# Row maxima of attention scores: one VectorE reduction over two PSUM banks, two such pairs and three ScalarE banks in place of three and four single ones

## The chip, the cores and the metric

One Trainium2 chip, one core of it. The metric is the device time of one execution in microseconds (us). The engines are TensorE (PE in the profile, PEld for its weight loads), VectorE (DVE), ScalarE (ACT), GpSimd (POOL) and SyncE (SP, which here issues transfers). The results of matrix products land in PSUM, which has 8 banks of 128 partitions x 512 f32 values. VectorE and ScalarE read them from there.

## The reference, cut to what matters

A differential attention layer followed by a routed feed-forward layer, each with a residual and a layer norm. The change touches the attention part alone:

```python
# x: 8 batches x 512 tokens x 128; 16 heads, 8 key/value heads, head size 4, two score maps per head
s = einsum('bthd,bshd->bhts', q, k) * scale
s = where(causal mask, s, most negative)
p = softmax(s, axis=-1)                        # needs the row maximum for safety
attn = einsum('bhts,bshd->bthd', p, v)
attn = attn1 - lambda_full * attn2             # then RMS norm, @ Wo, residual, layer norm
```

Behind it every token goes to one of 8 experts (the one with the largest router logit), and tokens are sorted by expert and run through the expert's weights in slots of 256 rows.

## The kernel before, in words

**Two passes over the scores.** The softmax subtracts each row's maximum before the exponential. So every score is computed twice: once with queries on the partitions ("natural", for the maxima, line 1393 on VectorE), and once with keys on the partitions ("turned", for the exponential, line 910 on ScalarE), where the maxima are fed into the product as extra rows of an operand. The maxima of a stage go VectorE (L1402, L1403: the maxima of pairs of halves, `mt`) -> GpSimd (split into three bf16 parts, `msplit`) -> TensorE (transposed, L743, the use `turn_max`) -> ScalarE (`mturn`) -> a transfer to memory and back into `qd`.

**Phases, steps and units.** The work of one batch is cut into 4 stages (`SUPER`), 32 stages in all (`NS`). In phase g the kernel takes the maxima of stage g and the exponentials of stage g - 2 (`LAG`). A phase has 9 steps t (`NC`), each of two units u = 2t and 2t + 1 (`NU` = 18). A unit is one PSUM bank of natural scores and one of turned scores, 128 x 512 each: a causal mask (L624 or L627 natural, L651 or L654 turned) and one or two products on top (L633 and L642 natural, L660 and L669 turned). The two units of a step use the upper and lower half of TensorE's rows and overlap partly. Behind the two units of a step TensorE takes the other uses of that step (list `uses(g, t)`) and the products of probabilities and values (L712, the "products").

**Three sets of banks.** The natural scores rotate through 3 banks (`NAT_RING`), which VectorE empties; three small uses that VectorE reads take a place in that rotation too (`wo`, `router`, `rank`). The turned scores rotate through 4 banks (`ST_RING`), which ScalarE empties, with `turn_max`, `turn_ot`, `turn_attn`, `turn_x1`, the projections `q`, `q2`, `k`, `k2` and `v` in the same rotation. The eighth bank (`pv_b`) gathers the products. TensorE waits before each filling until the bank's earlier content has been read: `s_nfree` counts VectorE's, `s_sfree` ScalarE's. TensorE takes its instructions in the written order, so a wait for either holds everything behind it.

**The jobs between.** VectorE's small work for a batch that is through with attention (`jobs_at`: `weigh`, `guess`, `stats`, `choose`, `chance`, `place`) is laid out by hand, one job after each unit's maximum. Most `choose`, `chance` and `place` jobs wait by semaphore for the job before them.

**What repeats.** With 4 stages to a batch, four kinds of phase follow one another. They are named here by what stands in them:

- phase with k (g = 5, 9, ...; for g = 21 VectorE's part lies at 324.42 to 340.24 us): projection `k` at step 2, `k2` at step 6, `wo` at step 8;
- phase with v (g = 22: 340.24 to 353.86 us): `stats` in steps 0 to 2, `v` at step 2, `weigh` in steps 5 and 6;
- phase with the router (g = 23: 353.86 to 368.46 us): `router` at step 2, `guess` from step 2 to 4, `choose` from step 4 to 8;
- phase with q (g = 20: 310.97 to 324.42 us, and g = 24: 368.46 to 381.91 us): `chance` at step 0, `rank` at step 2, `place` in steps 4 and 5, `q`, `q2` and `turn_attn`.

Every phase has `turn_max` at step 2 and `turn_ot` at step 4, and products in steps 0, 1, 3, 5, 6, 7 and 8.

After the 34 phases the feed-forward part runs over 23 slots; it uses the same eight banks under fixed numbers, and the change does not touch it.

## Time and profile before

| what | value |
|---|---|
| time, median of 3 runs | 680.28 us (674.95 to 680.87) |
| time of the profiled execution | 670.18 us |
| its span, first to last instruction | 667.7 us |
| busy: PE, DVE, ACT, POOL | 593.7, 539.6, 433.3, 415.3 us |
| TensorE clock granted, mean | 0.952 of full speed |
| phase with k, v, router, q (from one `mt` maximum to the next) | 15.82, 13.62, 14.60, 13.45 us |
| maxima of 128x512 (L1393) | 576, 369.2 us busy |
| exponentials of 128x512 (L910) | 576, 313.5 us busy |

A busy time counts when an engine had an instruction in work; VectorE's and ScalarE's records overlap a little with the next one, so the time from start to start is shorter than the record. The span is 2.5 us shorter than the time of the same execution. The time of the profiled execution stands 10 us under the median of the runs.

### The profile page before, as it was taken

How to read it: one execution, taken by the hardware profiler on the slowest of the kernel's cores; microseconds unless marked ns; L12 is line 12 of the kernel's file. 1: busy time of each engine (PE TensorE's matmuls, PEld its weight loads, DVE VectorE, ACT ScalarE, POOL GpSimd, SP SyncE). 2: the span in 40 equal slices, each digit the busy share in tenths (PEclk: the TensorE clock that was granted, in tenths of full speed). 3: DMA queues.
4: the chain of work that ended last, by engine and by line, in shares of the span. 5: the costliest groups of instructions: out<-in, count | busy, mean ns of one | idle time of the engine just before them, and what ended most of it. 6: DMA issues, size and time to landing. Idle time of an engine off the chain costs nothing.

```text
span 667.7 us, 19245 instructions
## 1 busy us (share of the span) xinstructions
PE 593.7 (89%) x6968; PEld 330.2 (49%) x6968; DVE 539.6 (81%) x1318; ACT 433.3 (65%) x903; POOL 415.3 (62%) x618
## 2 busy tenths in 40 slices
PE   3389899999989999998999999999988896999990
PEld 1134344344434444443444444343445785999990
DVE  6488988998998998899899889999746975666661
ACT  1105788887978887797888779787875343444441
POOL 6245257566877676687777668336363367687774
PEclk9576999999999999999999999999979996999995
DMA  3867566555664756666465655634129446465530
GB/s 112 262 211 246 159 197 217 165 177 183 186 197 123 231 162 190 202 183 194 113 229 167 213 190 166 192 115 117 46 60 329 138 137 189 136 196 189 196 125 24
DMA packets 70677, 114.54 MB, mean 172 GB/s; under 512 B 20028, under 2 KB 43068, under 8 KB 70300
## 3 DMA queue, kind: packets, MB, share of 16 engines
q1 hardware_dynamic: 58152, 76.22, 37.5%
q0 software_dynamic: 9168, 34.25, 14.9%
q10 hardware_dynamic: 3264, 2.85, 1.3%
q8 instruction: 55, 0.90, 0.6%
q14 instruction: 38, 0.31, 0.2%
HBM read 69.60 MB, written 47.27 MB: 175 GB/s over the span
## 4 chain that ended last, share of the span: by engine, by line
PE 53%; DVE 26%; DMA 6%; issue 6%; ACT 3%; POOL 2%; SPq 1%; ACTq 0%; POOLq 0%; DVEq 0%
DVE mr L1393 15%; PE bank L712 11%; PE bank L840 11%; PE bank L852 4%; PE bank L624 4%; PE bank L642 4%; PE bank L633 3%; DMA rows<-qk_parts 3%; PE bank L720 2%; PE bank L749 2%; PE bank L660 2%; PE bank L669 2%; PE bank L723 2%; ACT work L910 1%; PE bank L759 1%
## 5 line engine op out<-in xcount | busy, mean ns | idle before, releaser
L1393 DVE TENSOR_REDUCE mr<-bank 128x8 f32<-128x512 f32 x576 | 369.2, 681 | 43.7 <-PE bank L642 26.8
L910 ACT ACTIVATE work<-bank 128x512 f32<-128x512 f32 x576 | 313.5, 602 | 72.5 <-PE bank L669 51.4
L712 PE MATMUL bank<-work,v_aug 128*32 128x512 f32 (+7 forms) x2048 | 170.9, 418 | 0.0
L642 PE MATMUL bank<-rows 64*128 64x384 bf16 (+7 forms) x512 | 144.1, 292 | 0.0
L633 PE MATMUL bank<-rows 64*128 64x128 bf16 (+7 forms) x512 | 140.9, 293 | 0.0
L669 PE MATMUL bank<-qd,kz 64*128 64x384 bf16 (+7 forms) x512 | 137.0, 286 | 0.0
L660 PE MATMUL bank<-qd,kz 64*128 64x128 bf16 (+7 forms) x512 | 133.8, 287 | 0.0
L624 PE MATMUL bank<-bits 64*128 64x128 bf16 x448 | 100.8, 227 | 9.6 <-DVE mr L1393 8.6
L624 PEld LDWEIGHTS bank<-bits 64*128 64x128 bf16 x448 | 41.8, 94 | 121.5 <-DVE mr L1393 107.3
L651 PE MATMUL bank<-bits 64*128 64x128 bf16 x448 | 97.3, 224 | 0.0
L840 PE MATMUL bank<-xr,rows 128*128 128x256 f32 x368 | 86.6, 390 | 5.2 <-DVE xr L1619 4.6
L840 PEld LDWEIGHTS bank<-xr,rows 128*128 128x128 f32 x368 | 70.3, 196 | 15.0 <-DVE xr L1619 5.1
L1024 ACT ACTIVATE apart<-bank 128x256 f32<-128x256 f32 x92 | 34.6, 382 | 58.0 <-PE bank L840 42.5
L712 PEld LDWEIGHTS bank<-work,v_aug 128*32 128x32 f32 x2048 | 45.0, 108 | 49.1 <-issue 21.5
L1103 POOL CAST msplit<-mt 128x32 bf16<-128x32 f32 x32 | 7.7, 240 | 90.1 <-DVE mt L1403 90.1
L1239 POOL DMA_INDIRECT out_dram<-kz,row_u x46 | 45.4, 987 | 14.0 <-issue 10.4
L1655 DVE TENSOR_TENSOR apart<-apart,bank 128x256 f32<-128x256 f32 x92 | 37.2, 418 | 18.0 <-ACT apart L1024 17.3
L660 PEld LDWEIGHTS bank<-qd,kz 64*128 64x128 bf16 x512 | 47.5, 96 | 6.0
L1184 POOL DMA_INDIRECT x_sorted<-x_all,pos_u x32 | 32.0, 1000 | 29.4 <-DVE pos_u L1483 21.9
L642 PEld LDWEIGHTS bank<-rows 64*128 64x128 bf16 x512 | 49.4, 97 | 0.3 <-issue 0.3
L633 PEld LDWEIGHTS bank<-rows 64*128 64x128 bf16 x512 | 48.7, 96 | 0.5 <-issue 0.2
L669 PEld LDWEIGHTS bank<-qd,kz 64*128 64x128 bf16 x512 | 47.2, 95 | 1.2
(177 smaller groups left out, 1006.1 us busy)
## 6 DMA issues: line engine op xcount, KB each, us to landing
qk_apart<-apart SPq DMA_DIRECT2D x54, 256.0 KB, 3.6
rows<-qk_apart SPq DMA_DIRECT2D x64, 192.0 KB
kz<-qk_apart SPq DMA_DIRECT2D x64, 192.0 KB
qk_parts<-parts SPq DMA_DIRECT2D x90, 128.0 KB, 2.9
qk_apart<-apart POOLq DMA_DIRECT2D x42, 256.0 KB, 3.9
rows<-qk_parts SPq DMA_DIRECT2D x64, 96.0 KB
qd<-qk_parts SPq DMA_DIRECT2D x64, 96.0 KB
x_sorted<-in_c_pad SPq DMA_DIRECT2D x9, 390.0 KB, 4.3
```

Source lines behind the costliest of these rows:

```text
L624: pe.matmul(bk[:, :].rearrange("p (n t) -> p n t", t=L)[:, NB - 1 - i:NB:i, :], ident_h[lo:lo + L, :], mask_h[lo:lo + L, :], start=True, s ...
L633: m = pe.matmul(bk[:, 0:wa], qz[lo:lo + L, kv, NB - 1 - i].rearrange("p j l -> p (j l)"), kd[lo:lo + L, kv, 0:wa], start=False, stop=True, ...
L642: pe.matmul(bk[:, wa:T], qz[lo:lo + L, kv, i - 1].rearrange("p j l -> p (j l)"), kd[lo:lo + L, kv, 0:T - wa], start=False, stop=True, skip ...
L651: pe.matmul(bk[:, :].rearrange("p (n t) -> p n t", t=L)[:, 0:NB - i + 1:NB - i, :], ident_h[lo:lo + L, :], turned_h[lo:lo + L, :], start=T ...
L660: m = pe.matmul(bk[:, 0:wa], kz[lo:lo + L, kv, i].rearrange("p j l -> p (j l)"), qd[lo:lo + L, kv, L * i:T], start=False, stop=True, skip_ ...
L669: pe.matmul(bk[:, wa:T], kz[lo:lo + L, kv, NB - i].rearrange("p j l -> p (j l)"), qd[lo:lo + L, kv, wa:T], start=False, stop=True, skip_gr ...
L712: m = pe.matmul(pv_b[32 * t:32 * t + 32, L * kb:T], v_aug[:, vb, kv + v, kb, :], cols, start=kb == 0, stop=True, skip_group_check=True)
L840: m = pe.matmul(banks[f][:, h * SLOT:(h + 1) * SLOT], wbuf[:, n, h * FFN + f * P:h * FFN + (f + 1) * P], xst[:, n % 2, :], start=h == 0, s ...
L910: nc.scalar.activation(prob[:, pos, r, :], st_b[no % ST_RING][:, :], ACT.Exp, scale=HD ** -0.5).then_inc(s_sfree, 1)
L1239: nc.gpsimd.indirect_dma_start(out=out, out_offset=bass.IndirectOffsetOnAxis(row_u[:, j, a:a + 1], 0), in_=ynorm[:, j % 2, a, :], in_offse ...
L1393: V.tensor_reduce(mr[:, s % 2, u % 2, i, i:i + NB], nat_b[no % NAT_RING][:, :].rearrange("p (n t) -> p n t", t=L), AX.X, ALU.max)\
L1655: V.tensor_tensor(u_s[:, j % 2, f, :], sa[:, f, :], banks[f][:, SLOT:2 * SLOT], ALU.mult)\
```

## The change

Four of the eight banks become two pairs, each one PSUM tensor of 128 x 2 x 512. The two units of a step go to the two halves of a pair, and one reduction takes the maxima of both. TensorE waits for a free pair before the first unit of a step only. The rotation of natural scores then has 2 places (each a pair) in place of 3, that of turned scores 3 in place of 4. A use by VectorE (`wo`, `router`, `rank`) takes a whole place, of which it fills one bank. VectorE's order changes with it: the maximum of both units, then the uses of the step, then both jobs of the step.

```diff
         for t in range(NC):
             if g < NS:
-                for u in (2 * t, 2 * t + 1):
-                    nat["max", g, u] = len(nat_at)
-                    nat_out += 1
-                    nat_at.append(nat_out)
+                nat["max", g, t] = len(nat_at)
+                nat_in += 2
+                nat_out += 1
+                nat_filled.append(nat_in)
+                nat_at.append(nat_out)
...
-NAT_RING, ST_RING = 3, 4
+NAT_RING, ST_RING = 2, 3
...
-        banks = [bank(f"bank{i}") for i in range(8)]
-        nat_b, st_b, pv_b = banks[0:3], banks[3:7], banks[7]
+        nat_b = [ctx.enter_context(nc.psum_tensor(f"pair{i}", [P, 2, 512], F32)) for i in range(NAT_RING)]
+        st_b, pv_b = [bank(f"bank{i}") for i in range(ST_RING)], bank("products")
+        banks = [pair[:, r, :] for pair in nat_b for r in range(2)] + st_b + [pv_b]
...
-                    nat_wait(pe, NAT_NO["max", g, u])
+                    if u % 2 == 0:
+                        nat_wait(pe, NAT_NO["max", g, u // 2])
                     nat_mask(g, u)
...
-                wait(dve, s_nat, no + 1)
-                V.tensor_reduce(mr[:, s % 2, u % 2, i, i:i + NB],
-                                nat_b[no % NAT_RING][:, :].rearrange("p (n t) -> p n t", t=L), AX.X, ALU.max)\
+                wait(dve, s_nat, NAT_IN[no])
+                V.tensor_reduce(mr[:, s % 2, :, i, i:i + NB],
+                                nat_b[no % NAT_RING][:, :, :].rearrange("p r (n t) -> p r n t", t=L), AX.X, ALU.max)\
                     .then_inc(s_nfree, 1)
...
-                for u in range(NU):
+                for t in range(NC):
                     if g < NS:
-                        row_max(g, u)
-                    if u % 2:
-                        for name, n in uses(g, u // 2):
-                            take(name, n)
-                    for name, b, k in jobs_at(g, u):
-                        job(name, b, k)
+                        row_max(g, t)
+                    for name, n in uses(g, t):
+                        take(name, n)
+                    for u in (2 * t, 2 * t + 1):
+                        for name, b, k in jobs_at(g, u):
+                            job(name, b, k)
```

On VectorE, in a phase with the router, from the router's logits to the `choose` jobs (steps 2 to 5; `ss`, `nv`, `nint`, `rinv` are the `guess` jobs, `rmax`, `less`, `coded` the first `choose` jobs). Before:

```order
L1418 TENSOR_TENSOR logit<-bank,rb_s 128x32 [waits s_rt,s_nat]
L1362 TENSOR_SCALAR ss<-ss 128x64 [waits s_ss]
L1393 TENSOR_REDUCE mr<-bank 128x8 [waits s_nat]
L1365 TENSOR_SCALAR nv<-ss 128x64 [waits s_ss]
L1393 TENSOR_REDUCE mr<-bank 128x8 [waits s_nat]
L1367 TENSOR_SCALAR nint<-ss 128x64
L1393 TENSOR_REDUCE mr<-bank 128x8 [waits s_nat]
L1371 TENSOR_SCALAR rinv<-nint 128x64 [waits s_newton]
L1393 TENSOR_REDUCE mr<-bank 128x8 [waits s_nat]
L1444 TENSOR_REDUCE rmax<-logit 128x4 [waits s_nfree,s_rt]
L1393 TENSOR_REDUCE mr<-bank 128x8 [waits s_nat]
L1447 TENSOR_TENSOR less<-logit,rmax 128x32 [waits s_rexp,s_rt]
```

The same stretch now:

```order
L1433 TENSOR_TENSOR logit<-pair,rb_s 128x32 [waits s_rt,s_nat]
L1374 TENSOR_REDUCE ss<-sq 128x64 [waits s_newton,s_post]
L1377 TENSOR_SCALAR ss<-ss 128x64 [waits s_ss]
L1408 TENSOR_REDUCE mr<-pair 128x2x8 [waits s_nat]
L1380 TENSOR_SCALAR nv<-ss 128x64 [waits s_ss]
L1382 TENSOR_SCALAR nint<-ss 128x64
L1408 TENSOR_REDUCE mr<-pair 128x2x8 [waits s_nat]
L1386 TENSOR_SCALAR rinv<-nint 128x64 [waits s_newton]
L1459 TENSOR_REDUCE rmax<-logit 128x4 [waits s_nfree,s_rt]
L1408 TENSOR_REDUCE mr<-pair 128x2x8 [waits s_nat]
L1462 TENSOR_TENSOR less<-logit,rmax 128x32 [waits s_rexp,s_rt]
L1465 TENSOR_TENSOR coded<-logit,rmax 128x32 [waits s_rt]
```

Two jobs now follow one another where each had a maximum ahead of it; `ss` (L1377) stands right behind the sum that it reads, and `coded` (L1465) right behind the `choose` job that it waits for by semaphore.

On TensorE, in a phase with v, from `turn_max` at step 2 to the two units of step 3. Before:

```order
L743 MATMUL bank<-bits,msplit 96x128 [waits s_msp,s_sfree]
L730 MATMUL bank<-wv_s,xt_s 128x64 [waits s_sfree]
L730 MATMUL bank<-wv_s,xt_s 128x64 x3
L624 MATMUL bank<-bits 128x2x64 [waits s_nfree]
L651 MATMUL bank<-bits 128x128 [waits s_sfree]
L633 MATMUL bank<-rows 128x64
L660 MATMUL bank<-qd,kz 128x64
L642 MATMUL bank<-rows 128x448
L669 MATMUL bank<-qd,kz 128x448
L624 MATMUL bank<-bits 128x2x64 [waits s_nfree]
L651 MATMUL bank<-bits 128x128 [waits s_sfree]
```

The same stretch now (`pair` is a natural bank, `bank` a turned one):

```order
L758 MATMUL bank<-bits,msplit 96x128 [waits s_msp,s_sfree]
L745 MATMUL bank<-wv_s,xt_s 128x64 [waits s_sfree]
L745 MATMUL bank<-wv_s,xt_s 128x64 x3
L638 MATMUL pair<-bits 128x2x64 [waits s_nfree]
L665 MATMUL bank<-bits 128x128 [waits s_sfree]
L647 MATMUL pair<-rows 128x64
L674 MATMUL bank<-qd,kz 128x64
L656 MATMUL pair<-rows 128x448
L683 MATMUL bank<-qd,kz 128x448
L638 MATMUL pair<-bits 128x2x64
L665 MATMUL bank<-bits 128x128 [waits s_sfree]
```

No matrix product moved. The second unit of a step no longer waits for VectorE, and each wait on `s_sfree` is now for the third place back where it was for the fourth.

## Rows read from the trace of the kernel before

**Rows 1.** The page, costliest groups: busy, mean ns of one, idle before.

```profile
L1393 DVE TENSOR_REDUCE mr<-bank 128x8 f32<-128x512 f32 x576 | 369.2, 681 | 43.7 <-PE bank L642 26.8
...
L624 PEld LDWEIGHTS bank<-bits 64*128 64x128 bf16 x448 | 41.8, 94 | 121.5 <-DVE mr L1393 107.3
```

**Rows 2.** Windows of four phases: k, v, router, q.

```profile
324.42:340.24 15.82, 15.82 (x233) 7.73 (x236) 12.85 (x23) 12.56 (x26) 11.33 (x17) 1.00 0.59 189
340.24:353.86 13.62, 13.15 (x181) 6.21 (x181) 13.30 (x32) 12.29 (x26) 11.73 (x16) 1.00 0.55 169
353.86:368.46 14.60, 13.89 (x191) 6.05 (x185) 14.55 (x34) 11.80 (x25) 10.21 (x21) 1.00 0.58 173
368.46:381.91 13.45, 12.31 (x183) 5.74 (x184) 12.13 (x26) 10.22 (x22) 9.29 (x12) 1.00 0.67 216
```

**Rows 3.** Groups by shape, VectorE: the same operation at two widths.

```profile
L1580 DVE TENSOR_TENSOR at<-on_s,rl 128x1024 f32<-128x1024 f32 x1 | 1.2, 1225 | 0.0
...
L1584 DVE TENSOR_TENSOR dif<-at 128x512 f32<-128x512 f32 x1 | 0.7, 693 | 0.0
```

**Rows 4.** Timeline of VectorE, behind the last maxima: start, duration.

```profile
479.53 0.18 DVE L1469 TENSOR_REDUCE rsum<-chance 128x4 f32<-128x32 f32 x1
479.74 0.18 DVE L1471 RECIPROCAL x_all<-rsum 128x4 f32<-128x4 f32 x1
```

**Rows 5.** Timeline of ScalarE, phase with k: exponentials of units 4-5 and 8-9.

```profile
328.60 1.08 ACT L910 ACTIVATE work<-bank 128x512 f32<-128x512 f32 x2
...
331.98 1.08 ACT L910 ACTIVATE work<-bank 128x512 f32<-128x512 f32 x2 [0.57 <-PE bank L669]
```

**Rows 6.** Timeline of TensorE, the same phase: `k`, unit 6, products of step 3, unit 11.

```profile
328.81 0.64 PE L720 MATMUL bank<-xr,wq_s 128*32 128x256 f32 x8
...
329.82 0.23 PE L651 MATMUL bank<-bits 64*128 64x128 bf16 x1
...
330.47 1.07 PE L712 MATMUL bank<-work,v_aug 128*32 128x512 f32 x8
...
332.99 0.22 PE L651 MATMUL bank<-bits 64*128 64x128 bf16 x1
```

**Rows 7.** Timeline of ScalarE, phase with v: exponentials of units 6 to 9.

```profile
346.18 2.07 ACT L910 ACTIVATE work<-bank 128x512 f32<-128x512 f32 x4
```

**Rows 8.** Timeline of TensorE, phase with v: turned masks of units 10 and 11.

```profile
347.42 0.23 PE L651 MATMUL bank<-bits 64*128 64x128 bf16 x1
...
347.81 0.23 PE L651 MATMUL bank<-bits 64*128 64x128 bf16 x1
```

**Rows 9.** Timeline of VectorE, phase with v, units 8 to 17 and `weigh`.

```profile
346.53 2.06 DVE L1393 TENSOR_REDUCE mr<-bank 128x8 f32<-128x512 f32 x3 [0.20 <-PE bank L642]
...
350.75 3.07 DVE L1393 TENSOR_REDUCE mr<-bank 128x8 f32<-128x512 f32 x5
353.86 0.29 DVE L1402 TENSOR_REDUCE mt<-mr 128x16 f32<-128x128 f32 x1
```

**Rows 10.** Timeline of VectorE, phase with the router, steps 6 to 8.

```profile
365.05 0.17 DVE L1455 TENSOR_REDUCE rtop<-place_f 128x4 f32<-128x32 f32 x1
365.15 0.68 DVE L1393 TENSOR_REDUCE mr<-bank 128x8 f32<-128x512 f32 x1
...
367.75 0.68 DVE L1393 TENSOR_REDUCE mr<-bank 128x8 f32<-128x512 f32 x1
368.46 0.29 DVE L1402 TENSOR_REDUCE mt<-mr 128x16 f32<-128x128 f32 x1
```

**Rows 11.** Timeline of VectorE, start of the phase with q.

```profile
310.97 0.29 DVE L1402 TENSOR_REDUCE mt<-mr 128x16 f32<-128x128 f32 x1
...
311.36 0.68 DVE L1393 TENSOR_REDUCE mr<-bank 128x8 f32<-128x512 f32 x1
```

**Rows 12.** Timeline of TensorE, start of the phase with q.

```profile
309.70 0.20 PE L627 MATMUL bank<-bits 64*128 64x64 bf16 x1 [0.49 <-DMA rows<-qk_parts]
...
315.62 1.06 PE L712 MATMUL bank<-work,v_aug 128*32 128x512 f32 x8
```

More of the change, by code:

```diff
@@ L424, in place, with filled @@
             if (name, n) in TAIL_NO:
[L425 removed]
+                return pv_b, TAIL_NO[name, n], s_tail, s_tfree
             if name in FOR_DVE:
[L427 to L428 removed]
+                return nat_b[NAT_NO[name, n] % NAT_RING][:, 0, :], NAT_NO[name, n], s_nat, s_nfree
+            return st_b[ST_NO[name, n] % ST_RING], ST_NO[name, n], s_st, s_sfree
+        def filled(eng, name, n):
+            if (name, n) in TAIL_NO:
+                eng.wait_ge(s_tail, TAIL_NO[name, n] + 1)
+            elif name in FOR_DVE:
+                eng.wait_ge(s_nat, NAT_IN[NAT_NO[name, n]])
+            else:
+                eng.wait_ge(s_st, ST_NO[name, n] + 1)
         def emptied(eng, name, n):
@@ L521, in row_operands @@
                 if s >= SUPER:
-                    wait(sp, s_nat, NAT_NO["max", s - SUPER, NU - 1] + 1)
+                    wait(sp, s_nat, NAT_IN[NAT_NO["max", s - SUPER, NC - 1]])
                 if dst is qz:
@@ L733, in use @@
             def use(name, n):
-                bk, done, no, _ = place(name, n)
+                bk, no, done, _ = place(name, n)
                 if (name, n) in TAIL_NO:
@@ L924, in take @@
                     return
-                bk, done, no, free = place(name, n)
-                wait(act, done, no + 1)
+                bk, _, _, free = place(name, n)
+                filled(act, name, n)
                 if name == "v":
@@ L1226, in _ @@
                     if g == PHASES - 1 and t == 5:
-                        wait(pool, s_nat, NAT_NO["max", NS - 1, NU - 1] + 1)
+                        wait(pool, s_nat, NAT_IN[NAT_NO["max", NS - 1, NC - 1]])
                         pool.wait_ge(s_es, 1)
@@ L1407, in take @@
                     return
-                bk, done, no, free = place(name, n)
-                wait(dve, done, no + 1)
+                bk, _, _, free = place(name, n)
+                filled(dve, name, n)
                 if name == "wo":
```

23 lines of the change are left out of this document (11 added, 12 removed).

## The prediction

> **What bounds the kernel now.** I read the costliest groups first. VectorE's maxima are 576 instructions and 369.2 us, and the largest idle time ahead of a natural mask on TensorE (107.3 us of PEld) ends with a maximum [rows 1]. That suggests VectorE. The windows of one batch's four phases correct this picture [rows 2]. With k, TensorE is busy for all of its 15.82 us and VectorE for 12.85: TensorE bounds it. With the router, VectorE is busy for 14.55 of 14.60. With v it is busy for 13.30 of 13.62, and TensorE for 13.15, so both are nearly full. With q neither is (12.13 and 12.31 of 13.45): the reader will see below that VectorE holds its first third and TensorE the rest. The four make 57.49 us, with TensorE busy for 55.16 and VectorE for 52.84. So even free maxima could take no more than 2.3 us from a batch. The granted clock is 1.00 in all four, and the change gives no reason to move it. The rest of the argument is who is late where, phase by phase.
>
> **What one merged maximum costs.** A single maximum has a record of 0.68 us, and five in a row take 3.07 [rows 9]: (3.07 - 0.68) / 4 = 0.60 us from start to start. The trace has no reduction of 1024 elements. Another VectorE operation goes from 693 to 1225 ns when its row goes from 512 to 1024 elements, 0.53 us more [rows 3]. So the merged record is 0.68 + 0.53 = 1.21 us and the distance to the next one 0.60 + 0.53 = 1.13, where two singles took 1.20. The saving is 0.07 us a pair, 0.63 us a phase of nine. The bounds are 0 (the fixed part was hidden by overlap anyway) and 2 x 0.681 - 1.215 = 0.147 us (it wasn't); I take 0.07, since it goes by distances, which is what a full engine lives by.
>
> The Trainium skill (VectorE: DVE Perf Modes, on the trn2 errata) says that memory latency is exposed between instructions, and that one large tile pays it once where many small ones pay it each time. Its table has 120 cycles at 0.96 GHz as the fixed part of a reading from PSUM, 0.125 us. By the page the pairs would save 288 x 0.125 = 36 us of VectorE, by the distances 288 x 0.07 = 20; the sum below goes by the distances.
>
> **What two jobs in a row cost.** A small job between two maxima moves the next one by 0.10 us (365.05 to 365.15) [rows 10]: its latency lies under the maximum behind it. A job that waits for the one directly before it starts 0.21 us after it [rows 4]. So every waiting second job costs 0.11 us more than it did between two maxima. I count four in the phase with the router (`ss` behind its sum, `choose` 2, 4, 6), one with v (`stats` 4), two with q (`chance` 1, `place` 1), none with k. An independent second job costs nothing more.
>
> **What the third ScalarE bank costs.** TensorE may fill a turned bank when ScalarE has read what stood there, now three places back. I set each filling against the end of the reading three places earlier; a start came 0.05 us behind the releasing end where TensorE waited before.
>
> With k, step 2: the places are units 4, 5, `turn_max`, `k`. The exponential of unit 4 ends at 328.60 + 0.60 = 329.20 [rows 5], `k` starts at 328.81 [rows 6]. It would have to wait until 329.25: 0.44 us. At step 5, unit 11 starts at 332.99 [rows 6], and unit 9 is read at 331.98 + 1.08 = 333.06 [rows 5]: 0.12 us. TensorE is full in this phase, so both go into its length: **+0.56 us**. Elsewhere in this phase a filling starts after that end. The bound below is zero, if ScalarE gets back ahead through its idle 0.57 us [rows 5]; but what it waits for there is TensorE.
>
> With q, unit 11 repeats the 0.12 us. With the router the same place is hidden, since TensorE waits for VectorE all the time.
>
> **Phase with v.** ScalarE is late here: it empties `v` in four pieces and reads units 6 to 9 from 346.18 to 346.18 + 2.07 = 348.25 [rows 7]. Unit 11 was filled from 347.81 [rows 8], under a rotation of four. Under three its turned mask starts at 348.30, and its natural products, which stand behind that mask on TensorE, end about 0.45 later (unit 10: mask at 347.42 [rows 8], maximum at 346.53 + 2.06 - 0.68 = 347.91 [rows 9]), at 348.75. The maximum of units 10 and 11 can't start before, where that of unit 10 alone started at 347.91: 0.84 us late, of which 0.39 is the second half of the pair (347.42 to 347.81) and the rest the bank. `v` itself must wait like `k` does; it moves the chain by about 0.1 more (estimate). Behind that VectorE is full until the next phase (units 10 to 17 and `weigh` from 347.91 to 353.86 [rows 9]), so the delay stays, less four pairs of 0.07. What VectorE saves in steps 0 to 3 is lost, since it then waited for TensorE anyway (0.20 us at 346.53 [rows 9]). Sum: 0.84 + 0.10 - 0.28 = **+0.66 us**.
>
> **Phase with the router.** VectorE is full: -0.63 for nine pairs, +0.44 for four waiting jobs. At its end the pair maxima (L1402) waited for the last single one: 367.75 to 368.46 is 0.71, 0.11 over the distance [rows 10]; now the last `choose` job stands between and hides this, -0.11. Sum: **-0.30 us**.
>
> **Phase with q.** Its start is held by VectorE, and TensorE comes free of it with the products of step 3. Before, these began 315.62 - 310.97 = 4.65 us after the pair maxima [rows 11, 12]. Now `rank` takes a whole pair, and units 6 and 7 may only be filled when the maximum of units 4 and 5 is done: pair maxima 0.39 (to 311.36 [rows 11]), step 0 1.13, the two `chance` jobs 0.31, step 1 1.13, step 2 1.21, release 0.05, together 4.22, and then both units, 0.65 (329.82 to 330.47 [rows 6]), so 4.87. That is +0.22, and with unit 11 **+0.34 us**. TensorE bounds the rest, which takes over what was late. The transfer that TensorE waited for at the phase's first mask (0.49 us at 309.70 [rows 12]) lands at its old distance from step 2 of the phase before; this stands under VectorE's lateness and adds nothing.
>
> **The sum.** Per batch 0.56 + 0.66 - 0.30 + 0.34 = +1.26 us. Six batches pass through all four phases under full load, 7.6 us. The first phases have no exponentials or jobs and gain some tenths, the last stages have no `v`, `k` or `q` and come out near zero; the feed-forward part is unchanged. So 670.18 + 7.5 = 677.7 us for the profiled execution, a factor of 1.011, and 688 on the median of 680.28.
>
> **The rivals.**
>
> 1. *VectorE's saving comes through* (faster). For it: VectorE's wait is the largest at TensorE [rows 1]. If ScalarE's three banks were enough everywhere, and the second half of a pair always there in time, a batch would change by -0.52 (v: -0.63 + 0.11), -0.30 (router) and about -0.1 to -0.4 (q), some -1.1 us, so -7 over the kernel: 673. Against it: the ends of rows 5 and 7 stand after the fillings of rows 6 and 8.
>
> 2. *The stalls are absorbed*. ScalarE shifts its readings so that the waits don't repeat, or one phase's lateness is another's slack. Half of the +1.26 or less: +2 us, 682. For it: the windows with q and v have 0.3 to 1.3 us in which either engine is idle [rows 2]. Against it: most of that idle time is on one engine while the other is full.
>
> 3. *The fixed part is saved whole*, 0.147 us a pair. The router's phase gives 0.7 more, the v phase 0.3 more: +0.2 a batch, +1.5 us, 682. That is what the skill's rule (same page and section) says in kind. Against it: singles already follow each other at 0.60 with records of 0.68, so part of that latency is overlapped.
>
> 4. *A held pair holds ScalarE too* (slower). The wait for a pair stands ahead of the turned scores of the step on TensorE. Where VectorE is full (v, router, q: first third), TensorE gets a pair only when a whole 1.21 us reduction is over, then fills two turned banks at once; ScalarE idles, then its three banks are full again. It decides if TensorE's other work of a step (products up to 1.07 us [rows 6]) no longer fits into the 1.13 + 0.2 that VectorE takes per step. Half a microsecond more in each of the router and q phases makes +2.2 a batch, +13 in all: 693.
>
> **How the numbers follow.** Forecast 0.42 (688, its own spread 684 to 692), rival 1 0.17, rival 2 0.20, rival 3 0.07, rival 4 0.14. About 1% is what a measurement of this kernel can tell from no change, that is 673.5 to 687.1. Slower: two thirds of the forecast and rival 4, 0.42. Faster: rival 1, 0.17. Within: the rest, 0.41. The range 674 to 696 leaves out half of rival 1 and the far end of rival 4.
>
> **What would show it.** The merged maximum at 1.21 us and 1.13 from start to start. Over the same four phases about 58.7 us, with the phase of k near 16.4, v near 14.3, router near 14.3, q near 13.8. On TensorE a new wait of 0.4 for an exponential ahead of `k`, and 0.1 at unit 11; in the phase with v a wait of about 0.5 on ScalarE at units 9 to 11. VectorE's idle time grows at step 5 of that phase. The forecast is wrong if TensorE shows no waits for ScalarE beyond those of now, or if the phase with k keeps its 15.82.

## The result: 0.5% slower

The changed kernel takes 680.48 us (median of 20 executions) against 677.83 of the kernel before (20, same chip): a ratio of 1.0053, 95% interval 1.0033 to 1.0073. The forecast was 1.011. The profiled execution took 677.35 us, span 675.4 (before: 670.18 and 667.7), clock 0.961.

The page of the changed kernel, costliest groups, answers [rows 1] (busy, mean ns of one, idle before):

```profile
L1408 DVE TENSOR_REDUCE mr<-pair 128x16 f32<-128x1024 f32 x288 | 346.8, 1218 | 67.8 <-PE pair L656 51.0
...
L638 PE MATMUL pair<-bits 64*128 64x128 bf16 x448 | 97.7, 227 | 13.9 <-DVE mr L1408 13.4
L665 PE MATMUL bank<-bits 64*128 64x128 bf16 x448 | 98.2, 224 | 2.4 <-ACT work L925 1.4
...
L665 PEld LDWEIGHTS bank<-bits 64*128 64x128 bf16 x448 | 41.0, 93 | 24.6 <-ACT work L925 16.2
```

Before, the masks on TensorE had these rows (natural, then turned):

```profile
L624 PE MATMUL bank<-bits 64*128 64x128 bf16 x448 | 100.8, 227 | 9.6 <-DVE mr L1393 8.6
...
L651 PE MATMUL bank<-bits 64*128 64x128 bf16 x448 | 97.3, 224 | 0.0
```

VectorE's maxima take 22 us less (346.8 where they took 369.2), and VectorE waits 24 us more ahead of them. TensorE did not wait less for it: its natural masks wait 13.9 us where they waited 9.6, and the turned masks (L665) now wait for ScalarE. Windows of the four phases k, v, router, q, against [rows 2] (length, then busy PE, PEld, DVE, ACT, POOL, clock, DMA):

```profile
330.90:347.12 16.22, 15.85 (x228) 7.56 (x226) 12.29 (x13) 12.25 (x25) 11.63 (x17) 1.00 0.50 165
347.12:361.68 14.56, 14.04 (x187) 6.82 (x189) 12.87 (x22) 12.77 (x27) 11.00 (x16) 1.00 0.54 172
361.68:375.53 13.85, 12.87 (x181) 6.19 (x177) 13.63 (x26) 10.66 (x23) 10.91 (x21) 1.00 0.59 174
375.53:389.52 13.99, 12.91 (x193) 6.02 (x186) 11.83 (x18) 10.87 (x23) 9.02 (x12) 1.00 0.65 213
```

They sum to 58.62 us where 57.49 stood: +0.40, +0.94, -0.75, +0.54, together **+1.13 a batch**. The forecast had +0.56, +0.66, -0.30, +0.34, together +1.26.

TensorE's timeline, first `k`, then the third step of the phase with q (start, duration, idle before and its releaser):

```profile
335.51 0.64 PE L735 MATMUL bank<-xr,wq_s 128*32 128x256 f32 x8 [0.36 <-ACT work L925]
...
378.60 0.19 PE L788 MATMUL pair<-chosen,tri 128*128 128x32 bf16 x1 [0.23 <-DVE mr L1408]
...
379.73 0.23 PE L638 MATMUL pair<-bits 64*128 64x128 bf16 x1 [0.84 <-DVE mr L1408]
```

The waits are where they were forecast: `k` for an exponential, units 6 and 7 behind `rank` for a whole pair. With v the turned masks wait for ScalarE. TensorE's weight loads first, then VectorE behind them:

```profile
354.15 0.09 PEld L665 LDWEIGHTS bank<-bits 64*128 64x128 bf16 x1 [0.29 <-ACT work L925]
...
354.64 0.42 PEld L764 LDWEIGHTS bank<-ident,ot 128*128 128x128 f32 x4 [0.32 <-ACT work L925]
```
```profile
352.49 1.23 DVE L1408 TENSOR_REDUCE mr<-pair 128x16 f32<-128x1024 f32 x1 [0.44 <-PE pair L656]
...
354.59 1.23 DVE L1408 TENSOR_REDUCE mr<-pair 128x16 f32<-128x1024 f32 x1 [0.88 <-PE pair L656]
```

### The profile page after: what moved, and what is told of

It reads as the page before. It is cut to its first block, busy times and chain, and to the rows that moved or that the text cites. A ratio compares the mean times of both kernels' runs of the same rounds, so it can differ in the third digit from the quotient of the medians.

```text
span 675.4 us, 18928 instructions
## 1 busy us (share of the span) xinstructions
PE 592.5 (88%) x6968; PEld 334.4 (50%) x6968; DVE 523.9 (78%) x1030; ACT 430.9 (64%) x903; POOL 415.1 (61%) x618
## 4 chain that ended last, share of the span: by engine, by line
PE 55%; DVE 23%; DMA 6%; issue 6%; ACT 5%; POOL 3%; SPq 1%; ACTq 0%; POOLq 0%; DVEq 0%
DVE mr L1408 14%; PE products L727 13%; PE pair L855 9%; PE bank L867 4%; PE pair L638 3%; PE pair L656 3%; PE bank L683 3%; PE pair L647 3%; ACT work L925 3%; PE bank L764 3%; PE bank L674 2%; PE bank L735 2%; DMA rows<-qk_parts 2%; PE bank L665 2%; PE bank L738 2%
## 5 line engine op out<-in xcount | busy, mean ns | idle before, releaser
L1408 DVE TENSOR_REDUCE mr<-pair 128x16 f32<-128x1024 f32 x288 | 346.8, 1218 | 67.8 <-PE pair L656 51.0
L727 PE MATMUL products<-work,v_aug 128*32 128x512 f32 (+7 forms) x2048 | 171.7, 419 | 0.0
L656 PE MATMUL pair<-rows 64*128 64x384 bf16 (+7 forms) x512 | 137.2, 293 | 0.0
L647 PE MATMUL pair<-rows 64*128 64x128 bf16 (+7 forms) x512 | 136.8, 294 | 0.0
L638 PE MATMUL pair<-bits 64*128 64x128 bf16 x448 | 97.7, 227 | 13.9 <-DVE mr L1408 13.4
L665 PE MATMUL bank<-bits 64*128 64x128 bf16 x448 | 98.2, 224 | 2.4 <-ACT work L925 1.4
L855 PE MATMUL pair<-xr,rows 128*128 128x256 f32 x368 | 86.7, 391 | 5.0 <-DVE xr L1634 4.4
L855 PEld LDWEIGHTS pair<-xr,rows 128*128 128x128 f32 x368 | 70.5, 197 | 14.7 <-DVE xr L1634 4.9
L727 PEld LDWEIGHTS products<-work,v_aug 128*32 128x32 f32 x2048 | 45.1, 108 | 49.2 <-issue 18.6
L665 PEld LDWEIGHTS bank<-bits 64*128 64x128 bf16 x448 | 41.0, 93 | 24.6 <-ACT work L925 16.2
L656 PEld LDWEIGHTS pair<-rows 64*128 64x128 bf16 x512 | 48.1, 98 | 0.2 <-issue 0.2
```

Of the source, the lines that this page charges most:

```text
L638: pe.matmul(bk[:, :].rearrange("p (n t) -> p n t", t=L)[:, NB - 1 - i:NB:i, :], ident_h[lo:lo + L, :], mask_h[lo:lo + L, :], start=True, s ...
L647: m = pe.matmul(bk[:, 0:wa], qz[lo:lo + L, kv, NB - 1 - i].rearrange("p j l -> p (j l)"), kd[lo:lo + L, kv, 0:wa], start=False, stop=True, ...
L656: pe.matmul(bk[:, wa:T], qz[lo:lo + L, kv, i - 1].rearrange("p j l -> p (j l)"), kd[lo:lo + L, kv, 0:T - wa], start=False, stop=True, skip ...
L665: pe.matmul(bk[:, :].rearrange("p (n t) -> p n t", t=L)[:, 0:NB - i + 1:NB - i, :], ident_h[lo:lo + L, :], turned_h[lo:lo + L, :], start=T ...
L727: m = pe.matmul(pv_b[32 * t:32 * t + 32, L * kb:T], v_aug[:, vb, kv + v, kb, :], cols, start=kb == 0, stop=True, skip_group_check=True)
L855: m = pe.matmul(banks[f][:, h * SLOT:(h + 1) * SLOT], wbuf[:, n, h * FFN + f * P:h * FFN + (f + 1) * P], xst[:, n % 2, :], start=h == 0, s ...
```

## The experiments

Two questions: is each term of the sum right, and why do the medians show half of the forecast? A label's letter stands for the chip: the kernel before took 710 to 714 us on those of x, y and b, and 677 to 679 on those of z and a. Each ratio is against the kernel before on the same chip.

| run | ratio to before, 95% interval | k | v | router | q |
|---|---|---|---|---|---|
| before, profiled | | 15.82 | 13.62 | 14.60 | 13.45 |
| x1, copy of before | 1.0068 (1.0029 to 1.0106) | 15.82 | 13.62 | 14.61 | |
| a1, copy of before | 1.0013 (0.9976 to 1.0050) | 15.82 | 13.62 | 14.59 | 13.46 |
| y1, the changed kernel | 1.0034 (0.9995 to 1.0074) | 16.23 | 14.56 | 13.84 | |
| a2, the changed kernel | 1.0059 (1.0029 to 1.0089) | 16.22 | 14.54 | 13.85 | 14.00 |
| x2, three turned banks | 1.0110 (1.0051 to 1.0170) | 16.39 | 14.54 | 14.61 | |
| x3, and four natural | 1.0074 (1.0032 to 1.0116) | 16.39 | 14.27 to 14.56 | 14.61 | |
| x4, order of the jobs | 0.9937 (0.9899 to 0.9975) | 15.82 | 13.55 | 14.86 | |
| a4, pair by two, first half early | 1.0171 (1.0118 to 1.0224) | 16.40 | 14.30 | 14.86 | 13.97 |
| a3, pair by two behind one wait | 1.0254 (1.0211 to 1.0298) | 16.22 | 14.82 | 14.86 | 14.25 |

Phases stand at full clock and without a halt (a standstill of TensorE, below); the empty cells had one in each traced phase at full load.

**Copies (x1, y1, a1, a2).**

> The kernel before once more, nothing changed. It measures what two copies of one kernel differ by, and how far a profiled execution stands from the median of the runs. The changed kernel lost 7.2 us from one profiled execution to the other (677.35 against 670.18) but only 0.53% (3.6 us) between the medians. Theory A (the profiled executions show the kernel's own length, and the unprofiled runs hide half of the loss under something that they alone have): this run's profiled time is again near 670, its median near 678. Theory B (chance in one profiled execution): the profiled time falls anywhere from 668 to 678. Ratio to the kernel before 0.997 to 1.003 in either case.

> The changed kernel once more, nothing altered, beside the kernel before on one chip. Two theories for why the medians moved by 0.53% and the phases of the two profiled executions by 1.13 us a batch (about 1%). A: by chance between executions; then the ratio comes near 1.011. B: many executions of the kernel before hold TensorE up for 2 to 4 us late in each phase with q, with no semaphore to wait for and with half the clock behind it (all four kernels of the last call did, at 713 us), and the changed kernel does so less. Then its profiled execution here shows fewer such gaps and the ratio is below 1.005 on a chip where the kernel before has them.

> A copy of the kernel before, for two things: how far two copies of one kernel come out apart when they run turn by turn on one chip, and the partner of the next three. If the ratio of 0.5% that was measured for the change is real and not what copies differ by, this one comes out at 1.000 within 0.002. Its stages: up to the first mt maximum 42 to 43 us, the first two phases together 30 to 31, the rest as the profile of before.

> A copy of the changed kernel. Three parts add to what the full phases cost, by my theory: five batches (g = 9 to 28), not six, pass through all four phases at full load, +1.1 us each, 5.5 in all; the part up to the first mt maximum and the first two phases give back 1 to 2 us (first mt 0.5 us earlier, second phase pair 0.5 to 1 shorter), the stretch behind the last mt maximum 0.6 to 0.9. Total +3 to +4 us, ratio 1.004 to 1.006. The rival (the edges give nothing, the measured 0.5% is noise about the true 0.8 to 1.1%): ratio 1.008 to 1.011.

The phases repeat to some 0.02 us. The totals don't: x1, the same kernel as before, came out 0.7% above it, a1 0.1%. So an interval of one comparison is too narrow by some tenths of a per cent. The changed kernel against before is 1.0053, 1.0034 and 1.0059 in three comparisons; one of them alone would not prove 0.5%, but all three point the same way. The rival of a2 (0.8 to 1.1%) is refuted at its upper end only. The gap of 10 us between the profiled execution of before and its median was chance: a1's profiled execution took 678.42, its median is 678.52. Theory B of y1 (the changed kernel halts less) is not borne out: its trace has phases with q of 17.8 to 19.1 us, that of x1 17.0 to 18.5.

**The banks alone (x2, x3).**

```diff
-NAT_RING, ST_RING = 3, 4
+NAT_RING, ST_RING = 3, 3        # x3: 4, 3
-        nat_b, st_b, pv_b = banks[0:3], banks[3:7], banks[7]
+        nat_b, st_b, pv_b = banks[0:3], banks[4:7], banks[7]    # x3: banks[0:4]
```

> The kernel before with three banks for ScalarE in place of four and three single natural banks as before, one bank unused. My theory (the third bank costs by TensorE's waits for exponentials): phase with k 15.82 to 16.3, phase with v 13.61 to about 14.1, phase with q +0.1, router 0; profiled time +6 to +7 us. Rival (the loss of the change comes from the pair's coarse grain, not from ScalarE's banks): all four phases within 0.1 of before, profiled time +1 at most.

> Four single natural banks and three for ScalarE: the changed kernel's division of the eight banks, but 576 single maxima, each waited for by itself, and VectorE's old order of jobs. Against the changed kernel it tells what merging and pairing do at equal banks. If the pair's grain costs (my terms of +0.39 in the phase with v and +0.22 in that with q), this kernel is faster than the changed one there: v near 14.1, q near 13.5, k 16.2, but 14.6 with the router. If merging gains more than its grain costs, it is slower than the changed kernel in all but k. Against the run with three and three banks it tells what a fourth natural bank gives: I expect 0 to -0.3 us a batch.

Windows of x2, k and v:

```profile
155.10:171.49 16.39, 16.03 (x233) 7.74 (x236) 12.85 (x23) 12.54 (x26) 10.65 (x16) 1.00 0.54 174
171.49:186.03 14.54, 13.74 (x181) 6.43 (x181) 13.33 (x31) 12.29 (x26) 11.71 (x16) 1.00 0.54 168
```

The third bank alone costs 0.57 with k (forecast 0.56) and 0.92 with v (forecast 0.55 for the bank). The difference with v begins at `v` itself, for which I had estimated 0.1:

```profile
175.12 1.10 PE L730 MATMUL bank<-wv_s,xt_s 128*128 128x64 f32 x8 [0.30 <-ACT work L910]
```

It starts 3.63 us after the `mt` maximum, before 3.17 (343.41), so 0.46 later; the turned mask of unit 9 then starts 1.02 later (7.11, before 6.09), where I had looked for the first wait at unit 11. A fourth natural bank (x3) gives back 0 to 0.3 with v and nothing with k: at the changed kernel's division of the banks, single maxima are equal or 0.3 faster with v (14.55 in the changed kernel), and 0.76 slower with the router.

With q the whole phase can't be compared, since each has a halt at its end. But its first part can: in the phases g = 12 to 24 of x2 the products of step 3 start 4.66 us after the `mt` maximum, as before, and those of step 5 at 7.69 where they started at 7.55. So the bank costs 0.14 there; the forecast had 0.12.

**The order of the jobs alone (x4).** Both maxima of a step, its uses, then both jobs, on the banks of before.

> The kernel before, banks and single maxima unchanged, with only VectorE's order of the changed kernel: both maxima of a step, then the uses, then both jobs. My price of 0.11 us for each waiting second job: phase with the router 14.60 to 15.0 (four of them), phase with v +0.1, with q +0.1, k 0. Profiled time +3 to +4 us. Rival (VectorE's queue hides this): no phase moves by more than 0.1.

Router +0.26 (forecast +0.44 - 0.11), k unchanged, v 0.06 shorter. In the router's phase this is a sum of more than my terms: before, the last job met a GpSimd operation and took 0.66 us (see b1), here 0.22. The total 0.6% under before has no undisturbed phase that shows it; x1 says how little such a total proves.

**The maxima (a3, a4).**

```diff
-                wait(dve, s_nat, NAT_IN[no])
-                V.tensor_reduce(... nat_b[no % NAT_RING][:, :, :] ...).then_inc(s_nfree, 1)
+                for r in range(2):
+                    wait(dve, s_nat, NAT_IN[no])          # a4: NAT_IN[no] - 1 + r
+                    m = V.tensor_reduce(... nat_b[no % NAT_RING][:, r, :] ...)
+                m.then_inc(s_nfree, 1)
```

> The changed kernel with the maxima of a pair taken by two reductions of 512 instead of one of 1024, both behind the same wait for the whole pair and with one release behind the second: the merging alone is undone, banks and order of jobs stay. My price for merging is 0.07 us a pair: the phase with the router (VectorE full) 0.63 longer, 14.5 where it was 13.84; the phase with q 0.2 to 0.3 longer (three pairs ahead of its wait), k unchanged at 16.22, v at 14.55 or up to 0.3 more. About +0.9 a batch, +5 us with the first phases, 1.007 over the changed kernel. The rival (the fixed part is saved whole, 0.147 a pair): router 15.1, q +0.5, +1.9 a batch.

> The same with the first reduction waiting for its own half only (one word of the wait's number), so that VectorE no longer waits for the second half. My forecast put 0.39 us of the phase with v on that second half: then v comes out 0.3 to 0.4 under the kernel with both behind one wait. The rival (the third bank alone costs the 0.94, as the kernel with three single turned banks had +0.93): v within 0.1 of it. Router and k unchanged by either; q 0 to 0.3 less, since the first pair of that phase is read sooner.

Windows of a3 (v, router, q) and of a4 (k, v, q):

```profile
171.42:186.24 14.82, 14.19 (x187) 6.88 (x189) 13.44 (x31) 12.85 (x27) 11.11 (x16) 1.00 0.56 167
186.24:201.10 14.86, 13.29 (x185) 6.14 (x177) 14.72 (x35) 11.17 (x24) 10.69 (x21) 1.00 0.60 175
201.10:215.35 14.25, 12.66 (x189) 6.05 (x185) 12.40 (x27) 10.62 (x22) 8.95 (x12) 1.00 0.59 188
```
```profile
274.32:290.72 16.40, 16.04 (x233) 7.75 (x236) 12.86 (x23) 12.53 (x26) 11.62 (x17) 1.00 0.52 172
290.72:305.02 14.30, 13.77 (x187) 6.74 (x189) 13.35 (x32) 12.58 (x27) 11.14 (x16) 1.00 0.59 180
...
260.35:274.32 13.97, 12.38 (x187) 5.81 (x184) 12.40 (x27) 10.34 (x22) 9.01 (x12) 1.00 0.57 183
```

From a4 to a3 only the wait for the second half is added: v +0.52 (forecast 0.39), q +0.28, k -0.18. From a3 to a2 only the merging: v -0.27 (forecast -0.28), q -0.25, k 0, and router -1.01, where my price of nine pairs was 0.63 and the rival's 1.3; another mechanism is in it (b1). On the whole merging is worth 693.3 - 680.4 = 12.9 us here, some 5 of them since TensorE's clock fell in four of a3's phases with q (1.4 each, last section); banks, grain and order cost more than that.

**Where the border of q and k lies.** The windows begin and end at VectorE's `mt` maximum, and the second half moves this mark against TensorE's work. TensorE's first mask in the phase with k of g = 21, before (the maximum at 324.42) and changed (330.90):

```profile
325.21 0.20 PE L627 MATMUL bank<-bits 64*128 64x64 bf16 x1
```
```profile
331.48 0.20 PE L641 MATMUL pair<-bits 64*128 64x64 bf16 x1
```

It comes 0.79 us after the mark before, in x2 and in a4, but 0.58 after it in the changed kernel and 0.51 in a3. So the last maximum of the phase with q waits 0.2 to 0.3 for its second half, which lengthens q and shortens k in the windows and costs TensorE nothing. Without this shift k is 0.61 longer (forecast 0.56) and q 0.33 (forecast 0.34). The wait behind `rank` shows it by itself:

```profile
380.38 1.06 PE L727 MATMUL products<-work,v_aug 128*32 128x512 f32 x8
```

The products of step 3 start 4.85 us after the maximum at 375.53; the forecast was 4.87, before it was 4.65.

**Where the router's gain came from (b1).** VectorE's `ss` job against GpSimd's copies into `apart`, two of 1.49 us in one row. The kernel before, then the changed one:

```profile
356.54 2.98 POOL L1090 COPY apart<-parts 64x1536 bf16<-64x1536 bf16 x2
...
358.63 0.94 DVE L1362 TENSOR_SCALAR ss<-ss 128x64 f32<-128x64 f32 x1
```
```profile
364.89 3.03 POOL L1105 COPY apart<-parts 64x1536 bf16<-64x1536 bf16 x2
...
366.39 0.20 DVE L1377 TENSOR_SCALAR ss<-ss 128x64 f32<-128x64 f32 x1
...
367.63 0.33 DVE L1380 TENSOR_SCALAR nv<-ss 128x64 f32<-128x64 f32 x1
```

Before, the job starts inside the second copy and ends at 359.57, 0.05 behind its end (359.52). In the changed kernel it starts 1.50 us after their start, between the two, and takes 0.20; `nv` then ends 0.04 behind them. All 24 phases with the router from g = 7 on in four traces (before, the changed kernel, a2, a3) fit: started 1.39 to 1.52 us after the start of the copies, 0.19 to 0.20 us; 1.62 to 2.09 after, 0.94 to 1.41. The Trainium skill (SBUF — State Buffer, Who interferes with whom) describes it: VectorE and GpSimd share a port pair, held by whoever comes first for a whole instruction, and VectorE needs it in a two-port mode or with two inputs from SBUF. The trace agrees that the job lasts until the copy ends (0.05 behind it); whether it ran in such a mode no row shows. b1 moves the five `guess` jobs one unit in the kernel before:

```diff
-JOBS = {..., "guess": (7, 4, 5), ...}
+JOBS = {..., "guess": (7, 5, 5), ...}
```

> The kernel before with its five guess jobs one unit later in the phase with the router (first behind unit 5, not 4). In every traced phase where the ss job starts over 1.55 us after the start of GpSimd's apart copies (two of 1.49 us), it ends 0.05 us after they do; where it started 1.39 to 1.52 us after (g = 15 to 27 of the changed kernel), it took 0.20. My theory (the phase with the router became 0.76 shorter by the ss job missing that copy, not by the merged maxima, which give 0.5 to 0.6 and lose 0.3 to second jobs): here, with single maxima and four turned banks, the ss record is 0.18, and the phase with the router falls from 14.60 to 13.9 or 14.1, where TensorE's 13.89 bounds it. The other three phases are unchanged (15.82, 13.62, 13.45). Total 2.5 to 3.5 us under the kernel before, ratio 0.995 to 0.997. The rival (the wait is for something else, or GpSimd's later Newton steps hold the next split): router stays at 14.6 or q grows by what router gives.

Window of that phase, then GpSimd and VectorE in its timeline:

```profile
306.26:319.87 13.61, 12.46 (x179) 5.85 (x175) 13.54 (x35) 10.75 (x23) 9.78 (x21) 1.00 0.61 179
```
```profile
308.95 2.98 POOL L1090 COPY apart<-parts 64x1536 bf16<-64x1536 bf16 x2
...
311.75 0.23 DVE L1362 TENSOR_SCALAR ss<-ss 128x64 f32<-128x64 f32 x1
```

14.60 to 13.61, by one number and with single maxima. Here too the job begins inside the copies, but 0.18 before their end. The 0.99 is more than `ss` gives: from its start to the next maximum it is 0.15 us where it was 0.86, so 0.71. The last job of the phase has two inputs and met another GpSimd operation before, and no longer does. Before (g = 19), then b1, GpSimd and VectorE:

```profile
309.24 1.07 POOL L1152 TENSOR_TENSOR dn<-dif,rinv 128x512 f32<-128x512 f32 x1
...
309.67 0.66 DVE L1462 TENSOR_TENSOR cnt<-cnt 128x8 bf16<-128x8 bf16 x1
```
```profile
319.29 1.08 POOL L1152 TENSOR_TENSOR dn<-dif,rinv 128x512 f32<-128x512 f32 x1
...
318.98 0.25 DVE L1462 TENSOR_TENSOR cnt<-cnt 128x8 bf16<-128x8 bf16 x1
```

It gives 0.41 (0.58 to the next maximum, now 0.17); the jobs between lose 0.13. So the cause, jobs that meet a GpSimd operation, is shown (that they meet in a port pair is told by the page, and no run here tells it from another shared path), and the gain is larger than the whole change gave this phase. (The forecast of 13.9 as TensorE's bound was wrong: in 13.61 TensorE is busy for 12.46.) k and v are unchanged. Over its seven phases from g = 7 on with the router b1 gains 0.6 to 1.0 us each, 5.9 in all or 0.8%. The total shows 0.9971 (0.9936 to 1.0007), so less, and not surely anything: this chip has the halts described below in the very next phases (q 16.8 to 18.6 us). The gain is shown for the phase, not for the kernel.

The merged kernel's -1.01 from a3 divides by the timelines: `ss` to the next maximum 1.18 us in a3, 0.11 in a2, -1.07; `nv` and `nint` +0.27; the last job, which takes 0.52 beside GpSimd's `dn` and 0.21 in a3, +0.29; the rest, -0.50, is nine pairs at 0.06 (from a pair's start to what follows it 1.19 in a3, 1.13 in a2).

**Other places and jobs (y2, y3, z3).** y2 has `k` and `v` at step 3; y3 spreads `guess` and `choose` so that only one of the four waiting pairs is left; z3 spreads `choose` alone and moves GpSimd's scatters of `sort` (indirect transfers that GpSimd issues) to the phase with k. y3 and z3 also start `stats` a unit earlier.

```diff
+BATCH_USES = [..., (3, "k", -3), (6, "k2", -3), (3, "v", -2)]                       # y2
+JOBS = {..., "stats": (9, 16, 6), ...}                                            # y3, z3: was (9, 17, 6)
+SPREAD = {"guess": [4, 6, 8, 10, 12], "choose": [5, 7, 9, 11, 13, 15, 16, 17]}      # y3
+SPREAD = {"choose": [4, 6, 8, 10, 12, 14, 16, 17]}; CHAIN "sort": (13, 2)           # z3
```

> The changed kernel with the projections k and v at step 3 in place of step 2, so that they no longer stand right behind turn_max in the rotation of three. My theory (0.44 us of TensorE's wait ahead of k belongs to the third place back): phase with k 16.22 to about 15.8; phase with v 14.55 to about 14.3. Rival (the wait only moves to the next filling, since ScalarE reads at its own pace): both phases within 0.1.

> The changed kernel with VectorE's small jobs laid out so that only one of the four waiting pairs of the phase with the router is left (guess and choose interleaved, one of each per step) and the stats jobs one unit earlier. If a waiting second job costs 0.11 us: router 13.84 to about 13.5, v -0.1. Rival (TensorE or the operand transfer ends the phase by then): router stays at 13.8, with TensorE's wait for the transfer grown at its end.

> The changed kernel with two things more: the choose jobs spread over units 4 to 17 of the router phase so that no two that wait for one another stand back to back (guess jobs stay where they are), and the sort scatters a phase later (step 2 of the phase with k). My theory: the router phase at 13.4 to 13.5 us (it was 13.84, less the hidden waits of 0.11 each and the stall at the ss job), v phase 14.4 to 14.55, no wait of TensorE for msplit in the phase with q, q phase near 14.0, sum of four near 58.2 plus the halt of some 2 to 3 us now in the phase with k; so the total about 0.5% above the next kernel and 1% under the changed one. Rival (spreading the jobs brings back GpSimd's lateness): q phase again over 16 us.

y2: v 14.44 (-0.11), where 14.3 was expected. k gains nothing, where 15.8 was expected: its one phase without a halt before it is 16.30 (y1 16.23), and behind a halt it is 15.99 at best where y1 has 15.90. TensorE's wait ahead of `k` (0.36) has become one of 0.21 at the next mask, and k is 0.07 to 0.09 longer: the rival, the wait only moves, holds there. And in three of its five phases with the router at full load (y1: in one) the `ss` job meets the copies, and the phase takes 14.92 to 14.94 where it takes 13.85 otherwise. GpSimd and VectorE, g = 15, where the job starts 1.55 us after the start of the copies:

```profile
253.35 2.98 POOL L1105 COPY apart<-parts 64x1536 bf16<-64x1536 bf16 x2
...
254.90 1.48 DVE L1377 TENSOR_SCALAR ss<-ss 128x64 f32<-128x64 f32 x1
```

Whether the moved projections or the chip's halts set that start is not shown. The total, 1.0018 (0.9976 to 1.0060), proves nothing either way. y3: router 13.42 as expected, but q 16.8 to 19.9, since the later `guess` makes GpSimd's split of the maxima late: TensorE waits 1.8 to 2.3 us for `msplit`. 1.0138 (1.0071 to 1.0204). z3: no such wait in q (14.01), router 14.14 where 13.4 was expected, v 14.4 to 15.05; 1.0073 (1.0044 to 1.0101). In both k is 0.19 longer (16.41), for which I have no cause.

**The halts of the x, y and b chips (y4, z1, z2, z4).** There TensorE stands still in each phase with q from g = 12 on. At g = 12 of x1 nothing shows what it waits for; at g = 16 it waits 3.75 us for a maximum, and VectorE itself stood for 5.24 us, so the halt is not TensorE's alone. x1, TensorE at g = 12 and VectorE at g = 16, then its windows of g = 12 and g = 17:

```profile
212.46 0.23 PE L624 MATMUL bank<-bits 64*128 64x128 bf16 x1 [2.22 <-issue]
```
```profile
275.01 2.48 DVE L1393 TENSOR_REDUCE mr<-bank 128x8 f32<-128x512 f32 x4 [5.24 <-remote]
```
```profile
198.15:215.16 17.01, 13.62 (x185) 6.31 (x185) 12.13 (x27) 10.46 (x22) 9.92 (x12) 0.95 0.63 201
...
277.53:295.68 18.15, 18.09 (x237) 8.38 (x229) 12.93 (x22) 12.36 (x25) 10.66 (x16) 0.89 0.41 139
```

Behind the halt the clock is at its lower level (1.2 GHz) for some us. y4 and z4 are the kernel before with the scatters a phase later, z1 and z2 the two kernels with those of five batches at the end of the last attention phase (and without GpSimd's wait for them in between).

```diff
-          "chances": (11, 6), "rank": (12, 2), "sort": (12, 6)}
+          "chances": (11, 6), "rank": (12, 2), "sort": (13, 2)}        # y4, z4
-                wait(pool, s_scat[0], 16 * NI * (bn - 3))                   # z1, z2
-                    if b is not None:
+                    if b is not None and b > 4:                         # z1, z2
+                    if g == PHASES - 1 and t == NC - 1: for b in range(5): sort(b)
```

> The kernel before with the four scatters of the sorted rows (GpSimd, L1184) moved from step 6 of the phase with q to step 2 of the phase with k behind it. Theory B (TensorE's gap comes where these scatters run beside the loading of the next operands): the gaps leave the phase with q, which comes to 13.45 us, and on a chip that shows them the median falls by some per cent; on one without them nothing changes. Rival (the gap belongs to TensorE's place in its instruction stream, not to the scatters): it stays at step 8 of the phase with q.

> The kernel before with the sort scatters at step 2 of the phase with k, a second time, as the partner of z3 on this chip. Ratio to before as in its first run, 0.984 within 0.005; phases 13.45 with q, 18.4 to 19.8 with k. If the ratio comes out near 1.00 here, the gain of the first time belonged to that chip alone.

> The kernel before, with GpSimd's sort scatters of batches 0 to 4 moved out of the attention phases, into the last step of the last one (same number of scatters, all at the end, some tens of us of tail for the last batch's feed-forward part to wait for). My theory (the halt of TensorE in each phase with q, and the half clock behind it, comes with these scatters): every phase with q from g = 12 on is back at 13.45 us with no gap over 0.8 us on TensorE, and the four phases make 57.5 us a batch. The rival (the halt comes with something else of the phase, a transfer or the start of q): phases with q stay at 17 to 18.5 us. Total: the phases give back some 4 us in each of five batches, the tail costs about 20 to 30, so near the kernel before or up to 2% slower; the total is only a partner for the next kernel.

> The changed kernel with the same move of the scatters. With no halts in either, the medians of this one and of z1 differ by what the phases differ. My theory (the change costs 1.13 us a batch in full phases, hidden in the medians by halts and by what copies of one kernel differ by): phases 16.2, 14.55, 13.8, 14.0, sum 58.6, and the total 6 to 7 us above z1, 0.9 to 1.0%. The rival (the profiled phases overstate it, what is measured without the profiler is the 0.5%): the total at most 3.6 us above z1.

y4: q back at 13.45 to 13.50 in all batches, the halt now in k (18.4 to 19.9 us), 0.9843 (0.9798 to 0.9888). The halt goes where the scatters go. z4, the same kernel on another chip: 1.0121 (1.0076 to 1.0165). That chip has no halts to save, and the scatters cost TensorE 1.1 to 1.9 us of waiting for `msplit` with v. So the gain of y4 was that chip's. z1 against z2 is the change without halts in either: medians of 710.13 and 713.05, means apart by a ratio of 1.0054 (six runs each; 1.001 to 1.010), where I had expected 0.9 to 1.0%. Both carry some 33 us of scatters at the end.

## Why the prediction came out where it did

**Right: direction, place and most terms. Luck: their sum.** The +1.26 a batch came out as +1.13 because two misses nearly cancel: v cost 0.28 more than forecast, the router's phase 0.45 less. The forecast and what the runs showed, term by term:

- the merged maximum: record 1.21, measured 1.22; distance 1.13, measured 1.13; saving 0.07 a pair, measured 0.06. Rival 3 (0.147) is refuted for whole pairs in a row. The Trainium skill (VectorE: DVE Perf Modes, on the trn2 errata) would make it 0.125, and the measurement does not agree (its rule is told of SBUF, its table has the row for PSUM);
- the third bank with k: 0.56, and 0.57 by itself (x2). The window shows 0.40, since the mark between q and k moved by 0.21;
- with v: bank and `v` 0.55, measured 0.92 by itself (x2) and 0.68 beside pairs read by halves (a4). The mis-sized term is "about 0.1" for `v`: it starts 0.46 late. Second half 0.39, measured 0.52; merging -0.28, measured -0.27. Together 0.66, measured 0.94;
- with q: 0.34, in the window 0.54, of which 0.21 is the moved mark, so 0.33. The wait behind `rank` is there (0.84 us) and makes +0.20 (forecast +0.22), unit 11 0.13 (forecast 0.12);
- with the router: order +0.33, measured +0.26, an agreement that is partly luck, since in x4 the last job no longer meets `dn`; pairs -0.63, measured -0.50. The rest of -0.75, another -0.51, is the `ss` job missing GpSimd's copy (-1.07) less what `nv` and the last job lose beside GpSimd (+0.56). This cause stood in no term: I had put VectorE's meetings with GpSimd at nothing, without a reason. Where the job meets the copy (g = 11 of the changed kernel) the phase takes 14.94, more than before.

**Wrong: "Six batches pass through all four phases under full load, 7.6 us", and that the ends add nothing.** This step made the forecast of 1.011 twice the measured 1.0053. By the profiled executions (before, a1, z1 against changed, a2, z2), stretch by stretch:

| stretch | forecast | measured, mean of each |
|---|---|---|
| up to the first `mt` maximum | some tenths less | 42.31 to 41.95: -0.4 |
| g = 1 to 8 | 5 phases (24 less 19), +1.6 less some tenths | 111.9 to 111.4: -0.5, the copies of before 5 us apart, of changed 2 |
| g = 9 to 27 at full load | 19 phases, +6.0 | 275.7 to 281.0: +5.4 |
| g = 28 to 31 (without z1, z2) | near zero | 53.2 to 53.6: +0.4 |
| behind the last maxima (without z1, z2) | near zero | 189.0 to 187.6: -1.3 |

-0.4 - 0.5 + 5.4 + 0.4 - 1.3 = +3.6 us, what the ratio of 1.0053 says too; single executions lie several us apart, so this agreement is one of size. Of the +5.4, 5.1 is what 19 undisturbed phases differ by; fallen clocks and waits for transfers make the rest. Full load stood for five phases of each kind but q (four), 19 phases, not 24: the forecast lost 0.6 us by the size of those, 2 by calling five of the first phases full, and 1.3 behind the last maxima, where ScalarE's last exponential ended 26.1 us after the last `mt` and now ends after 25.0. I counted batches by number and not by which of their phases had the jobs and exponentials that fill the engines. The first eight phases are too unsteady (granted clock 0.63 to 0.88 in the first two) to say more than that nothing shows them to add.

**The rivals.** Rival 1 is refuted, k, v and q are all longer. Rival 2 named the right size of the total by the wrong cause: nothing is absorbed within a batch. Rival 4's mechanism (a held pair holds ScalarE) shows in the waits behind `rank`, not in the phase with the router.

**Open.** Why only some chips show the halts beside the scatters, how x1 and x4 came to differ by 1.3% with equal undisturbed phases, and what behind the last maxima ScalarE gained from.

## What to carry to other kernels

Merging two reductions pays only on an engine that is late; banks come from somewhere, and the reader that loses one pays (0.57 and 0.92 us a phase for 0.06 a pair). Price a steady phase, then count with care how many phases really are steady, the edges by themselves. Before a small VectorE job is priced by its own work, look what GpSimd does in that instant: moving five jobs by a unit gave 0.99 us a phase, twice what nine merged maxima gave. And where phases are measured from one engine's mark, see whether that mark moved against the other engine before giving a wait to one phase or the next.

## What the hardware showed that was not expected

- A 128x64 VectorE operation took 0.18 to 0.24 us, or up to 1.48 where it began inside a GpSimd copy and lasted until the copy's end; 0.03 us decided it (a start 1.52 us after the copies' start: 0.20; 1.55 after: 1.48).
- Behind two short waits in the phase with q (0.5 and 0.84 us) TensorE's clock fell in some executions and not in others, in the same kernel. With the changed banks it fell in 3 of 12 such phases (g = 12 to 24 of the changed kernel, a2, z2), in a3 and in a4 (0.57 and 0.91 us in a3) in 3 of 4; in before, a1 and z1 in none of 12. Each costs 1.4 us. Windows of 1 us, a3, then z2, third figure from the end is the clock:

```profile
325.00:326.00 1.00, 0.44 (x7) 0.12 (x1) 1.00 (x3) 1.00 (x3) 1.00 (x2) 1.00 1.04 399
326.00:327.00 1.00, 0.29 (x5) 0.19 (x5) 1.00 (x2) 0.29 (x2) 1.00 (x2) 1.00 0.87 332
...
329.00:330.00 1.00, 1.00 (x12) 0.36 (x10) 0.26 (x1) 0.00 (x0) 0.46 (x1) 0.50 0.71 172
```
```profile
378.00:379.00 1.00, 0.29 (x5) 0.19 (x5) 1.00 (x1) 0.40 (x2) 1.00 (x1) 1.00 0.95 363
379.00:380.00 1.00, 0.81 (x16) 0.51 (x20) 0.28 (x3) 0.29 (x1) 1.00 (x2) 1.00 1.04 395
380.00:381.00 1.00, 1.00 (x8) 0.00 (x0) 1.00 (x1) 0.79 (x2) 1.00 (x2) 0.50 0.76 267
```

- TensorE's halts of 1 to 4 us beside GpSimd's scatters, on some chips only, some with VectorE standing too.
